# Causal attention, cross attention and experts of a six-layer decoder block, laid out anew

## The reference, cut to what matters

```
x += L0_attn(ln(x))     # linear attention, 4 heads, and a feed-forward part: not touched
x += L0_xattn(ctx, ln(x), mask)
    q = ln @ Wq.T; k, v = [ctx_n @ Wkv.T ; ln @ Wlkv.T]      # 64 context keys and 1024 own keys
    attn = softmax(where(mask, rmsnorm(q) * SCALE @ rmsnorm(k).T, -max))   # 4 heads of 64
    out = (attn @ v) @ Wo.T + bo
x += L0_ffn(ln(x))      # gated recurrence: not touched
x += L1_attn(ln(x))
    score = q @ k.T                                          # 16 heads of 16, with biases
    attn = softmax(where(causal, score, -inf) / sqrt(16))
    out = (attn @ v) @ Wout + bout
x += L1_xattn(ln(x), ctx)   # 16 heads over 64 context keys: not touched
x += L1_ffn(ln(x))
    # top-2 of 8 experts, 8 groups of 256 tokens, at most 64 tokens of a group for an expert
    expert_inputs = einsum('GSEC,GSM->EGCM', dispatch, x)
    hidden = gelu(expert_inputs @ w0) * (expert_inputs @ w1) # 256 -> 1368
    out = einsum('EGCM,GSEC->GSM', hidden @ wo, combine)
```

## Time and profile before

| | us |
|---|---|
| median of 3 runs | 2447.39 (2447.15 to 2449.5) |
| span of the profiled execution | 2485.0 |
| PE busy / DVE / ACT / POOL in it | 2163.5 / 1206.4 / 764.6 / 36.2 |
| mean granted PE clock in it | 0.885 of 2.4 GHz |

### The profile page before, as it was taken

The page is one execution under the profiler, slowest core; times in us unless marked ns, Lnnn a source line. Parts: engine busy times, 40 slices in busy tenths (PEclk is TensorE's granted clock), DMA queues, the critical chain, the costliest instruction groups (busy, mean ns, idle before and its releaser), DMA issues. The chain is left out here.

```text
span 2485.0 us, 31033 instructions
## 1 busy us (share of the span) xinstructions
PE 2163.5 (87%) x10906; PEld 1609.2 (65%) x10962; DVE 1206.4 (49%) x2231; ACT 764.6 (31%) x1507; POOL 36.2 (1%) x54
## 2 busy tenths in 40 slices
PE   6877868999799977875999789997865999999998
PEld 4335325877488743333999679983544887888786
DVE  4124035365435642124878468774545443444443
ACT  2313144122412221133555345552223221121111
POOL 0000001000100000000000000000001000000000
PEclk8999966599857988987999989998986898989999
DMA  3010000000000000007220132200020111111100
GB/s 136 0 46 0 0 3 1 0 1 1 1 1 1 1 0 0 0 14 156 35 36 1 26 45 43 27 2 2 0 91 0 46 69 68 68 68 68 68 1 34
DMA packets 29885, 72.12 MB, mean 29 GB/s; under 512 B 3320, under 2 KB 14520, under 8 KB 27320
## 3 DMA queue, kind: packets, MB, share of 16 engines
q1 hardware_dynamic: 29752, 70.40, 10.6%
HBM read 62.00 MB, written 8.39 MB: 28 GB/s over the span
## 5 line engine op out<-in xcount | busy, mean ns | idle before, releaser
L1298 PE MATMUL psum<-arena 128*128 x2304 | 286.8, 276 | 0.0
L1298 PEld LDWEIGHTS psum<-arena 128*128 128x128 f32 x2304 | 272.2, 193 | 9.7 <-issue 0.7
L1339 ACT ACTIVATE arena<-psum,b_nm 128x128 f32<-128x128 f32 (+7 forms) x256 | 188.0, 739 | 255.8 <-DVE arena L1389 183.1
L1370 DVE TENSOR_REDUCE b_mx<-psum 128x1 f32<-128x640 f32 (+7 forms) x176 | 180.7, 1027 | 51.7 <-PE psum L1269 45.9
L847 ACT ACTIVATE arena<-psum,x_nm 128x1024 f32<-128x1024 f32 x64 | 71.3, 1114 | 336.8 <-PE psum L772 306.1
L791 PEld LDWEIGHTS psum<-arena,x_turned 128*128 128x128 f32 x1024 | 148.6, 231 | 21.1 <-issue 20.0
L1281 PE MATMUL psum<-ident,arena 128*128 128x128 f32 x1152 | 158.6, 277 | 3.3 <-ACT arena L1339 3.2
L1378 DVE COPY arena<-psum 128x512 f32<-128x512 f32 x176 | 121.7, 691 | 73.8 <-PE psum L1281 73.6
L791 PE MATMUL psum<-arena,x_turned 128*128 128x64 f32 x1024 | 156.0, 318 | 0.8 <-DVE x_turned L907 0.8
L1985 PE MATMUL psum<-m_wo,arena 128*128 128x256 f32 (+1 forms) x704 | 153.4, 379 | 0.0
L907 DVE COPY x_turned<-psum 128x512 f32<-128x512 f32 (+1 forms) x192 | 102.3, 551 | 104.6 <-PE psum L772 104.0
(11 more groups left out here) (336 smaller groups left out, 3347.3 us busy)
## 6 DMA issues: line engine op xcount, KB each, us to landing
m_w<-w SPq DMA_DIRECT2D x16, 1368.0 KB, 8.7
m_wo<-wo SPq DMA_DIRECT2D x8, 1280.0 KB
b_q_stack<-b_q_dram SPq DMA_DIRECT2D x64, 128.0 KB, 4.9
b_k_stack<-b_k_dram SPq DMA_DIRECT2D x64, 128.0 KB, 8.5
weights_sb<-weights SPq DMA_DIRECT2D x2, 2820.0 KB, 9.2
weights_sb<-weights SPq DMA_DIRECT2D x1, 3328.0 KB, 13.0
xT<-x_t SPq DMA_DIRECT2D x2, 1024.0 KB, 10.3
out<-xT SPq DMA_DIRECT2D x4, 512.0 KB, 3.1
```

The costliest lines, as they stand in the source:

```text
L1298: mm = pe.matmul(out_bank(u)[:, i * WIDE:(i + 1) * WIDE], turned[u % 2][:, n, :], v_all[:, bass.ds(b * (TT * D) + kb * D + first, WIDE)], ...
L1339: ins = act.activation(probs[u % 2][:, at], score(u)[:, at], ACT.Exp, bias=nm[:, u % 4, i:i + 1], scale=SCALE, accum_out=rs[:, u % 4, i:i ...
L1370: dve.tensor_reduce(mx[:, u % 4, 0:nh], unit.spread(score(u)), AX, ALU.max).then_inc(s["row_max"].sem)
```

## The change

The three layers are written anew; the others are as before.

**Cross attention.** The exponentials are computed with keys on partitions, so that the probabilities are the moving operand of the value matmul and need no transpose. The row's maximum is still taken with queries on partitions (`piece`, two heads on rows 0 to 63 and 64 to 127, plain f32 now), one step ahead, and is brought across as two bf16 rows (`turn_shift`) that a two-row matmul adds to the scores. The row sums come from matmuls with a block of ones. Both batches are projected ahead of the one loop over 8 steps of 9 slots.

```diff
+    STEPS = B * NCH * FT          # 8: batch, half of the queries, pair of heads
+    GROUPS = TT + 1               # 9 slots: 8 blocks of own keys, one of context keys
+                def piece(n, i):
+                    to = tile(("piece", n, i))
+                    for h in range(PAIR):
+                        rows = slice(h * DH, (h + 1) * DH)
+                        mm = pe.matmul(to[:, h * CH:(h + 1) * CH], qt[b][rows, m, q0:q0 + P], kt_[b][rows, m, first:first + CH],
+                                       start=True, stop=True)
...
+                def scores(slot):
+                    if slot >= 1:
+                        pe.wait_ge(*s["expd"](slot))
+                    for h in range(PAIR):
+                        pe.matmul(to[0:keys, h, :], ones16[h * DH:h * DH + 2, 0:keys], shift_t[h * DH:h * DH + 2, n % 2, :],
+                                  start=True, stop=False)
+                    for h in range(PAIR):
+                        mm = pe.matmul(to[0:keys, h, :], k, qt[b][rows, m, half * CH:(half + 1) * CH], start=False, stop=True)
+                def values(slot):
+                    if kt == 0 and n >= 1:
+                        pe.wait_ge(*s["out_copied"](n))
+                    for h in range(PAIR):
+                        mm = pe.matmul(out_tile[h * DH:(h + 1) * DH, :], v, probs[slot % RING][0:keys, h, :],
+                                       start=(kt == 0), stop=(kt == TT))
+                    if kt % 2 == 1:
+                        for back in (1, 0):
+                            for h in range(PAIR):
+                                group = PAIR * (1 - back) + h
+                                mm = pe.matmul(den_tile[group * 32:(group + 1) * 32, :], ones[:], probs[(slot - back) % RING][:, h, :],
+                                               start=(kt == 1), stop=(back == 0 and kt == TT - 1))
...
+                for slot in range(SLOTS):          # PE's order
+                    scores(slot)
+                    if n + 1 < STEPS and kt < 7:
+                        for i in (0, 1) if kt == 0 else (kt + 1,):
+                            piece(n + 1, i)
...
+                    if slot >= 1:
+                        values(slot - 1)
+                    ins = act.activation(probs[slot % RING][:], two_heads(units), ACT.Exp, scale=SCALE)     # ACT, each slot
+                    if n >= 1 and kt == 1:
+                        copy_out(n - 1)
+                dve.tensor_reduce(mx[...], two_heads(tile(("piece", n, i))), AX, ALU.max)                    # DVE, each piece
+                dve.reciprocal(den_inv[:], tile(("den", n))[:, 0:CH])                                        # DVE, once a step
```

```diff
-    QPART = (0, 0, 0, 1, 1, 1, 2, 2)
-    KPART = (0, 1, 2, 0, 1, 2, 0, 1)
+Q_PART = (0, 0, 0, 1, 1, 2)
+K_PART = (0, 1, 2, 0, 1, 0)
...
+                def keep_shift(hs):                # SP
+                    sync.wait_ge(*s["read"](nth["shift", hs] + 1))
+                    for i in range(SHIFT):
+                        sync.dma_start(qs[hs // 2 % 3][ROWS + i:ROWS + i + 1, :, half * CH:(half + 1) * CH],
+                                       stage[i * QUAD:(i + 1) * QUAD, hs % 2, :]).then_inc(shifted[hs % 2].sem, 16)
...
+                def scores(slot):
+                    if slot >= SCORES:             # 3 banks
+                        pe.wait_ge(*s["expd"](slot - SCORES + 1))
+                    mm = pe.matmul(score(slot)[:, 0:n], ks[a][0:ROWS + SHIFT, h, ki * P:(ki + 1) * P],
+                                   qs[a][0:ROWS + SHIFT, h, q0:q0 + n], start=True, stop=not diagonal)
+                def values(pair):
+                    for i in range(2):
+                        for h in range(QUAD):
+                            mm = pe.matmul(out_tile[h * PAD:(h + 1) * PAD, CH - n:CH], v_aug[:, b * TT + ki, quad * QUAD + h, :],
+                                           probs[(QUAD * (2 * pair + i) + h) % RING][:, 0:n],
+                                           start=(ki == 0), stop=(ki == 4 * half + 3))
...
+                for slot in range(QUAD * len(groups)):     # PE's order, 384 slots
+                    scores(slot)
+                    more_pieces(upto[slot], upto[slot + 1])
+                    if x == QUAD - 1 and ki % 2 == 1 and slot // QUAD >= 3:
+                        values(slot // QUAD // 2 - 1)
```

```diff
+                def gather(g, m):                  # 8 groups x 2 feature tiles
+                    for t in range(2):
+                        mm = pe.matmul(c.bank(n % BANKS), xn_tok[:, 2 * g + t, m * P:(m + 1) * P], one_hot[:, g % 2, t, :],
+                                       start=(t == 0), stop=(t == 1))
...
+                for ex in range(EXP):
+                    widen(ex)
+                    if ex % 2 == 0:
+                        if ex:
+                            combine(ex // 2 - 1)
+                        turn_back(ex // 2)
+                    narrow(ex)
+                combine(PAIRS - 1)
...
+                    if ex + 1 < EXP:               # ACT, behind the expert's gelus
+                        act.wait_ge(*e["w1_done"](HT * (ex + 1)))
+                        split_x(ex + 1)
+                        split_weights(ex + 1)
```

More of the change, by code:

```diff
@@ L542, in cross_attention_layer @@
+    order += [("den", STEPS - 1), ("project", STEPS - 1)]
+    nth = {what: n for n, what in enumerate(order)}
     with ExitStack() as ctx:
         norm_s = signals(nc, ctx, "xn", norm_signals())
[L544 to L547, removed]
@@ new lines, in value, with tile @@
+                def value(b, i):
+                    bank = room(b, "v", i)
+                    for t in (0, 1):
+                        first = b * S + (2 * i + t) * P
+                        for k in range(FT):
+                            mm = pe.matmul(bank[:, t * D:(t + 1) * D], xn_all[:, k, first:first + P], c.w("x_wlkv", k, D, D),
+                                           start=(k == 0), stop=(k == 1))
+                    mm.then_inc(s["v"].sem)
+                def tile(what):
+                    n = nth[what]
+                    if n >= 2:
+                        pe.wait_ge(*s["read"](n - 1))
+                    return ring_tile(what)
@@ L1091, in causal_attention_layer, with part_of @@
-    U = len(units)
-    more = [u for u in range(U) if len(units[u].blocks) > 4]
-    nth2 = {u: n for n, u in enumerate(more)}
+    STEPS = B * QUADS
+    HALVES = 2 * STEPS
+    ROWS, SHIFT = len(Q_PART) * DH, 2
+    LOADS = 2 * len(Q_PART) * 16
+    PAD = 32
+    RING = 16
+    SCORES, TILES = 3, 4
+    pieces = score_pieces()
+    NPC = len(pieces)
+    NPC_0 = sum(qi < 4 for qi, *_ in pieces)
+    LATER = 6
+    def part_of(hs):
+        return hs // 2 // QUADS, hs // 2 % QUADS, hs % 2
+    groups = [(hs, ki) for hs in range(HALVES) for ki in range(4 * (hs % 2) + 4)]
@@ new lines, in causal_attention_layer @@
+    upto = count_pieces()
+    assert upto[-1] == NPC * STEPS
+    order = []
+    for slot in range(-1, QUAD * len(groups)):
+        for p in range(upto[slot] if slot >= 0 else 0, upto[slot + 1]):
+            order.append(("piece", p))
+            if turned_after(p) is not None:
+                order.append(("shift", turned_after(p)))
+        if slot >= 0:
+            (hs, ki), x = groups[slot // QUAD], slot % QUAD
+            if hs >= 1 and ki == 3 and x == 1:
+                order.append(("out", hs - 1))
+            if hs == 2 * QUADS + 1 and ki in (0, 2):
+                order.append(("turn" if ki == 0 else "project", 0, x))
@@ new lines, in project, with more_pieces @@
+                def project(b, x):
+                    m, j = divmod(x, NCH)
+                    bank = tile(("project", b, x))
+                    pe.wait_ge(*s["read"](nth["turn", b, 3] + 1))
+                    for k in range(FT):
+                        mm = pe.matmul(bank, c.w("b_wo", k, m * P, P), ot[:, k, j * CH:(j + 1) * CH], start=(k == 0), stop=(k == 1))
+                    mm.then_inc(s["made"].sem)
+                def more_pieces(first, last):
+                    for p in range(first, last):
+                        piece(p)
+                        if turned_after(p) is not None:
+                            turn_shift(turned_after(p))
@@ L1180, in _ @@
+                values(len(groups) // 2 - 1)
+                turn_out(HALVES - 1)
+                for x in range(4):
+                    turn_batch(B - 1, x)
+                for x in range(4):
+                    project(B - 1, x)
             @block.scalar
```

1699 lines of the change are left out of this document (905 added, 794 removed).

## The result

| | before | after | forecast |
|---|---|---|---|
| median of 3 executions, us | 2447.39 | 1980.98 (1980.04 to 1983.06) | 1945 (1870 to 2180) |
| span of the profiled execution | 2485.0 | 1979.3 | 1974 |
| mean granted PE clock | 0.885 | 0.941 | |

The ratio is 0.807 (95% interval 0.801 to 0.814): 466 us less. The forecast's direction and mechanism came out; its time is 36 us too low. Further executions on three chips moved the reference, not the result: before took 2447 to 2488 us in 33 more executions, with 0.882 to 0.903 as mean clock, the changed kernel 1978.8 to 1981.3 in four more (ratio 0.798, 0.795 to 0.802). One of the three chips gave both 2447 and 2488 us, so the spread is not one between chips.

What follows compares the result with a forecast made beforehand. TensorE (PE) was taken to set the end of all three stages; savings of 157 + 265 + 89 = 511 us from 2485 left a span of 1974, times 0.985 = 1945 us, range 1870 to 2180.

Steps and rivals of the forecast that it cites:

- cross: ahead of the loop, loop, tail: Cross attention: 121 us ahead, 38.5 x 8 = 308 in the loop, 12 behind; stage 441 against 598, -157 us.
- causal: ahead, loop, tail: Causal attention: loop at 87 us, eight steps of 31 make 248, tail 14; stage 349 against 614, -265 us.
- experts: to the gather, gather and split, loop and end: Expert layer: norm and routing 73 us, then 35.6, eight experts 434, end 7; stage 550 against 639, -89 us.
- Full overlap of column parts: Both attention loops: matmuls on column parts run beside each other, two or four for the price of one.
- rival C: Both attention loops: columns don't overlap; cross +152 us, causal +176, span 2302, time 2267; chance 0.11.
- Rivals B: Both attention loops: columns overlap only in program order; +76 us cross, +67 causal, span 2117, time 2085; chance 0.13.
- The scaling: Whole kernel: profiled execution is 1.5% above the median, so the 1974 us span times 0.985 gives 1945 us.
- The prediction's 0.2%: Whole kernel: the difference a measurement can tell; faster by over 0.2% got chance 0.96.
- what now lies between and behind the loops goes: Causal attention: 614 - 73.5 - 2 x 259 = 22 us between and behind the old loops was taken to disappear.
- The changes between parts: Cross loop: 3.5 changes between parts of the array in a slot, 0.17 us each, 5.4 us a step.
- The wait for `copy_out`: Cross loop: once in a step the values of slot 0 wait for the step before's `copy_out`, 1.5 us.
- Rival D: Cross loop: half of the new loop runs at a granted 0.50; +148 us, span 2122, time 2090; chance 0.13.

Runs made afterwards that it cites:

- head-by-head kernel: Changed kernel with the loop over heads made the outer one in causal attention's `values`, against a rerun of the changed kernel (1979.5 us): 1984.0 us.

## Why the prediction was right, and where its sizes were off

| step of the forecast | forecast | measured |
|---|---|---|
| cross: ahead of the loop, loop, tail | 121, 308, 12 | 115.7, 297.5, 15.2 |
| causal: ahead, loop, tail | 87, 248, 14 | 87.7, 273.6, 16.4 |
| experts: to the gather, gather and split, loop and end | 78.5, 30.1, 441 | 68.4, 32.5, 441.7 |
| the three stages | 441, 349, 550 | 428.4, 377.7, 542.6 |
| span | 1974 | 1979.3 |
| time | 1945 | 1981.0 |

- **Full overlap of column parts** was chosen between ends 328 us apart (rival C), on rows that show only the other cut. It held: 1.00 us for four quarters, 1.86 for a group of 16, and 6.99 without it. The choice was made by likeness, and nothing in the rows of before decided it. Rivals B and C each fell to one run.
- **The scaling was the largest error, 30 us.** The sum was right to 5 us in spans, and that closeness is luck: causal attention took 29 us more than its term, cross attention 13 less, experts 7 less, and the layers that were not touched 4 less. Then I multiplied by 0.985 because the profiled execution was above the median of three. The surplus was not a property of the profile: those three executions were at the low end of a spread from 2447 to 2488 us, and the changed kernel doesn't share the spread. Its parts that I could trace (11.3 of 17 us) belong to the old expert layer, which was about to be replaced. Without the factor the forecast is 1974, 0.4% off. The prediction's 0.2% as what a measurement of this kernel can tell was too small for the kernel before, whose executions spread by 1.6%.
- **The causal loop was 26 us short.** Its steady pace, 31.45 us, is the forecast's 31 and gives 3.6 in eight steps. Missing altogether was the first batch's end: "what now lies between and behind the loops goes". It doesn't; its transposes and 8 f32 matmuls only move into step 4, 9.3 us, nearly all PE time (40.2 of 40.7). They are a term of the sum that was never written down. By the windows the first step costs 15.0 us over the pace and the last gives back 4.0: the maxima run some 36 tiles ahead of the scores, of which I had counted only the 12 ahead of the loop. So the first step has 64 maxima for 38, DVE is busy for 40.1 us in it and not 25.2, PE waits 3.0 us for the DMA of a shift, and the clock is granted at 0.90; how the 15 us divide among these isn't shown. Step 7 is another 1.7. Together that is the 25.6 us.
- **Cross attention was 13 us shorter.** The changes between parts were taken as 0.17 us. By starts they are 0.10 each for the shift (0.32 - 0.22), for the scores and for the maxima (0.96 - 0.86), 0.15 for the values: 4.7 us a step for 5.4. The wait for `copy_out` was forecast at 1.5 us and is 1.27 in seven of eight steps, and it was PE's only one of size in the loop. That is 9 of the 10.5 us of the loop. Ahead of it the norm took 25.2 us for 30, context, projections and what follows on them 72.8 for 71, maxima and shift 17.7 for 20; behind it 15.2 for 12.
- **Experts were 7 us shorter**: ahead of the gather 10 less than forecast (68.4 for 78.5), gather and split 2.4 more. Of the 73 us of norm and routing taken as unchanged, the block ahead of the norm shrank from 12.0 to 7.5 us; from the norm's end to the gather it is 38.6 us (1466.5 to 1505.1), where the sum had 39 for routing and 5.5 for one-hots and a cold start. The pace, 30.59 + 19.01 + (6.91 + 1.75)/2 = 53.93, was forecast as 54.0.
- **Rival D, the clock**, stays out: the loop has 0.99. How near it was, no row of before could say; with the maxima of two heads on the same rows 0.50 was granted for 51 us, 27 of them in the loop (435.8 to 463.3). And the clock has a larger part in the gain than the forecast said. By the earlier trace rows the old loop did 352 PE records in 105 us at 0.50 and 748 in 118 at 1.00; at the second stretch's pace the 352 would take 55.5, so each batch lost about 50 us by this estimate. Of the 169 us won in cross attention some 100 are therefore the clock that the new loop is granted (0.99) and only some 70 are work taken away. Both were in the forecast's terms, since they were priced at full clock; which was which was not said.

Two statements of the Trainium skill bear on it (TensorE: Matmul & The Clock Gate, Part 3). The 2.38 times for three column tiles is less than what these layers show, 3.76 for four: 0.79 for each tile against 0.94. The rule that matmuls start in program order does not hold here between parts: in the head-by-head kernel the second head's first matmul starts 14 ns after the first head's, ahead of the first head's other one.

## What to carry to other kernels

Probabilities as the moving operand, with narrow outputs laid beside each other in the columns of the array, trade many short products and their transposes for a few long ones; here one matmul per set of parts plus 0.10 to 0.15 us for each change of parts gave the price. A factor between a profile and a median may only be applied once it is known in which stage it arises, above all if that stage is being replaced. When a loop is merged or moved, write down every instruction that the old version had between its rounds and say where each one is now.

## What was not expected of the hardware

Each column part takes its matmuls in its own order: even with one head's four passes written ahead of the next head's, the first passes start 14 ns apart. The old cross loop was granted 0.50 for the same 105.8 us at each of its two starts, in all four traces, with PE 94% busy; the new one recovered within 6 us of its start after a pause of 20 us, and with its pairs of 64-row matmuls one after the other 0.50 was granted for 51 us around its start. In none of these cases is it shown why.
